# Attention 0 of a four-layer kernel: the gate's multiplication is moved from VectorE to GpSimd, with a second buffer

## The chip, the core and the metric

The kernel runs on one core of a Trainium2 chip. The metric is the device time of one execution in microseconds (us); the median of three runs is compared. In the rows of the profile the engines are PE (TensorE's matmuls), PEld (TensorE's weight loads), DVE (VectorE), ACT (ScalarE), POOL (GpSimd) and SP (SyncE).

## What is computed

The reference is a chain of four layers, each an attention and a feed-forward part, over 16 sequences of 256 rows with 128 channels. Only attention 0 and the first step of feed-forward 0 matter here:

```python
Q, K, V = (x @ Wq.T + bq), (x @ Wk.T + bk), (x @ Wv.T + bv)      # 16 heads of 64
scores = einsum('bnhd,bmhd->bhnm', Q, K) * (SCALE * adaptive_scale)
w = softmax(scores); attn = einsum('bhnm,bmhd->bnhd', w, V)
y = x + (attn @ Wo.T + bo)
x = layernorm(y) * gamma + beta        # the wrapper adds x and normalises once more
...
logits = einsum('td,ed->te', tokens, gate_w)      # feed-forward 0: 8 experts
```

The kernel works out these logits at the end of attention 0, on vector engines: each row of the new x (128 channels) times each of the 8 rows of gate_w, then a sum over the channels.

## The kernel before

Attention 0 is the function attention_wide. All float32. A batch is one sequence of 256 rows, that is two row tiles (t = 0, 1) of 128; a unit is a pair of heads of one batch, so there are 8 units in a batch and 128 in all. The engines run the same loop over **slots**, one slot for a unit, and each engine does in a slot what `at(slot, ...)` and `pair(slot, ...)` give it, in the order of its code. That order is the whole schedule: an engine that waits holds up all that stands behind it. With batch b, the offsets are

```python
LAG_T, LAG_PV, LAG_O = 2, 5, 6
X_AT, V_AT, Y_AT = -6, -1, U + 4
Z_AT, A_AT, W_AT = Y_AT + 4, Y_AT + 5, Y_AT + 8
G_AT = W_AT + 1
```

with U = 8, so Y_AT is 12, Z_AT 16, A_AT 17, W_AT 20 and G_AT 21.

- TensorE: in an even slot it scores two units (L272); in an odd slot it multiplies two units by V (L299) and then projects one quarter of a batch's V (L263, 64 of them, the last in slot 125). In each slot it turns a unit's probabilities (L285, unit slot-2) and projects Q and K of unit slot+2 (L255). Projections, turned x and the output projection (L307) all go through the one PSUM bank A_M; `bank_free` makes each wait until VectorE or ScalarE has emptied it. So the V projection of an odd slot waits for VectorE's take_qk (L410) of the even slot before it.
- VectorE, even slot: four row maxima (L399), then what falls due (take_y L429 with its moments L419/L422, write_x L448, inner_norm L437, outer_stats L419/L422), then take_qk (L410). Odd slot: the reciprocal of the even unit's sums (L404), take_turned (L415), take_qk (L410), the reciprocal of the odd unit's sums (L404). Behind that stand gate_x (L457, in slots 8b+21, +23, +25, +27, all odd) and sum_logits (L462, one slot later each).
- GpSimd, each slot: normalise (L185, four instructions for a unit, waits for the reciprocal). Behind it in odd slots: the reciprocal root of the first moments (root, L198/L200, slot 8b+15), add_biases of the next batch (L193, L194, slot 8b+17 counted from the batch before it) and affine (L205, L208, slot 8b+17), the root of the second moments (slot 8b+19).
- ScalarE: exponentials (L355), and copies out of PSUM.

Two places come up again. **Place A**, slot 8b+16: inner_norm (L437) waits for the root of slot 8b+15, and take_qk stands behind it. **Place B**, slot 8b+18: outer_stats (L419) waits for affine's last instruction (L208) of slot 8b+17, and take_qk stands behind it.

gate_x writes the one buffer `gated` (128 x 512) and waits until the sum before it has read it.

Of the kernel before, what the change touches and what calls it, by code (L numbers as in the profile page):

```python
# [9 lines left out]
ALU = mybir.AluOpType  # L10
ACT = mybir.ActivationFunctionType
AX = mybir.AxisListType
P = 128
H = 16
NB, SEQ = 16, 256
TB = SEQ // P
# [3 lines left out]
E = 8  # L20
# [30 lines left out]
def attention_wide(nc, name, x_state, x_rows, consts, w, dram, onward):  # L51
# [10 lines left out]
    G_AT = W_AT + 1  # L62
# [3 lines left out]
    with ExitStack() as ctx:  # L66
        def sb(n, shape, dt=F32):
            return ctx.enter_context(nc.sbuf_tensor(f"{name}_{n}", shape, dt))
# [17 lines left out]
        y, z, s = sb("y", [P, 2, TB, P]), sb("z", [P, 2, TB, P]), sb("s", [P, 2, TB, P])  # L86
        stats, mv, rstd = sb("stats", [P, 2, TB, 6]), sb("mv", [P, 2, TB, 2]), sb("rstd", [P, 2, TB])
        veps, mhalf = sb("veps", [P, TB]), sb("mhalf", [P, TB])
        gates, gated = sb("gates", [P, E, P]), sb("gated", [P, E // 2, P])
        CLEAR = 8  # L90
        CLEARS = max(TILES.values()) // CLEAR
        zeros, zeroed, cleared = sb("zeros", [P, CLEAR, P]), sem("zeroed"), sem("cleared")
# [4 lines left out]
        gate_done, lg_out = sem("gate_done"), sem("lg_out")  # L97
# [17 lines left out]
        def after(eng, signal, count):  # L115
            if count > 0:
                eng.wait_ge(signal, count)

        def at(s, offset, batches=NB):

            b, r = divmod(s - offset, U)
            return b if r == 0 and 0 <= b < batches else None
# [22 lines left out]
        def by_vector(n):  # L145

            return n % 2 == 1
# [6 lines left out]
        with nc.Block() as block:  # L154
# [19 lines left out]
            @block.gpsimd  # L174
            def _(pool):
                nc.gpsimd.memset(zeros[:], 0.0).then_inc(zeroed, 1)
                nc.gpsimd.memset(mhalf[:], -0.5).then_inc(set_up, 1)
                pool.wait_ge(set_up, 1)
                pool.wait_ge(in_rest, IN_REST)

                def normalise(n):
                    pool.wait_ge(inverted, n + 1)
                    for j in range(2):
                        for t in range(TB):
                            nc.gpsimd.tensor_scalar(prob[:, n % NP, j, t, :], prob[:, n % NP, j, t, :], rinv[:, n % NP, j, t:t + 1], 1.0,  # L185
                                                    ALU.mult, ALU.mult).then_inc(normed, 1)

                def add_biases(b):
                    pool.wait_ge(x_in[b // XB], 16)
                    after(pool, y_out, TB * (b - 1))  # L190
                    after(pool, s_out, TB * (b - 1))
                    xv = x_state[:, TB * b:TB * (b + 1), :]
                    nc.gpsimd.tensor_tensor(xb[:, b % 2], xv, bo[:].unsqueeze(1).to_broadcast([P, TB, P]), ALU.add).then_inc(xb_ready, 1)  # L193
                    nc.gpsimd.tensor_tensor(xbeta[:, b % 2], xv, beta[:].unsqueeze(1).to_broadcast([P, TB, P]), ALU.add).then_inc(xb_ready, 1)  # L194

                def root(b, moments, done):
                    pool.wait_ge(moments, 2 * TB * (b + 1))
                    nc.gpsimd.tensor_scalar(veps[:], mv[:, b % 2, :, 1], EPS, None, ALU.add).then_inc(done, 1)  # L198
                    pool.wait_ge(done, 2 * b + 1)
                    nc.gpsimd.tensor_tensor(rstd[:, b % 2], veps[:], mhalf[:], ALU.pow).then_inc(done, 1)  # L200

                def affine(b):
                    pool.wait_ge(z_out, TB * (b + 1))
                    pool.wait_ge(xb_ready, 2 * (b + 1))
                    nc.gpsimd.tensor_tensor(z[:, b % 2], z[:, b % 2], gamma[:].unsqueeze(1).to_broadcast([P, TB, P]), ALU.mult).then_inc(s_out, 1)  # L205
                    pool.wait_ge(s_out, TB * b + 1)
                    after(pool, x_done, TB * (b - 1))
                    nc.gpsimd.tensor_tensor(s[:, b % 2], z[:, b % 2], xbeta[:, b % 2], ALU.add).then_inc(s_out, 1)  # L208

                for slot in range(FIRST, LAST + 1):  # L210
                    if (n := pair(slot)) is not None:
                        normalise(n)
                    if (b := at(slot, Y_AT - 3)) is not None:
                        add_biases(b)
                    if (b := at(slot, Z_AT - 1)) is not None:
                        root(b, y_stats, rooted)
                    if (b := at(slot, A_AT)) is not None:
                        affine(b)
                    if (b := at(slot, W_AT - 1)) is not None:
                        root(b, s_stats, rooted2)  # L220
# [165 lines left out]
            def _(dve):  # L386
# [61 lines left out]
                        nc.vector.tensor_scalar(x_state[:, TB * b + t, :], s[:, b % 2, t, :], mv[:, b % 2, t, 0:1], rstd[:, b % 2, t:t + 1],  # L448
                                                ALU.subtract, ALU.mult).then_inc(x_done, 1)

                def gate_x(b, q):
                    t, some = q // 2, slice(E // 2 * (q % 2), E // 2 * (q % 2 + 1))
                    if b == 0 and q == 0:
                        dve.wait_ge(in_rest, IN_REST)
                    dve.wait_ge(x_done, TB * b + t + 1)
                    after(dve, lg_out, 2 * TB * b + q)
                    nc.vector.tensor_tensor(gated[:], x_state[:, TB * b + t, :].unsqueeze(1).to_broadcast([P, E // 2, P]), gates[:, some, :], ALU.mult).then_inc(gate_done, 1)  # L457

                def sum_logits(b, q):
                    t, some = q // 2, slice(E // 2 * (q % 2), E // 2 * (q % 2 + 1))  # L460
                    dve.wait_ge(gate_done, 2 * TB * b + q + 1)
                    nc.vector.tensor_reduce(onward["logit"][:, TB * b + t, some], gated[:], AX.X, ALU.add).then_inc(lg_out, 1)  # L462

                for slot in range(FIRST, LAST + 1):
                    if slot % 2 == 0:
                        for n in two(slot):
                            row_max(n, 0)
                            row_max(n, 1)
                    if slot % 2 == 1 and (n := pair(slot, 1)) is not None:
                        invert(n)  # L470
                    if (n := y_half(slot)) is not None:
                        take_y(n)
                    if (b := at(slot, W_AT)) is not None:
                        write_x(b)
                    if (b := at(slot, Z_AT)) is not None:
                        inner_norm(b)
                    if (b := at(slot, A_AT + 1)) is not None:
                        outer_stats(b)
                    if (n := pair(slot, LAG_T)) is not None and by_vector(n):
                        take_turned(n)  # L480
                    if (n := pair(slot, -QK_AHEAD)) is not None:
                        take_qk(n)
                    if slot % 2 == 1 and (n := pair(slot)) is not None:
                        invert(n)
                    for q in range(2 * TB):
                        if (b := at(slot, G_AT + 2 * q)) is not None:
                            gate_x(b, q)
                        if (b := at(slot, G_AT + 2 * q + 1)) is not None:
                            sum_logits(b, q)

# [2401 lines left out]
```

## Time and profile before

| | us |
|---|---|
| median of 3 runs | 2697.12 |
| lowest, highest | 2694.36, 2703.2 |
| the profiled execution | 2692.44 |
| its span in the profile | 2690.7 |
| span busy: TensorE matmul | 2248.2 (84%) |
| span busy: VectorE | 1593.5 (59%) |
| span busy: ScalarE | 1572.2 (58%) |
| span busy: GpSimd | 1361.9 (51%) |
| mean granted TensorE clock | 0.911 |

Attention 0 fills the first 684 us or so of the span: its last instruction, a sum of logits on VectorE, starts at 683.57. The timeline lists instructions of one engine in order of time, neighbours of one line merged with their count (x4), and in brackets how long the engine sat idle before and what ended that. The view of waits sums such idle times by pairs: who waited, for whom.

### The profile page before, as it was taken

To read this page: it belongs to the slowest core of one execution; us is meant where nothing else is said; L and a number is where in the kernel's file an instruction comes from. 1 tells how busy PE (TensorE), PEld (TensorE's weight loads), DVE (VectorE), ACT (ScalarE), POOL (GpSimd) and SP (SyncE) were. 2 spreads that over 40 slices of the span, in tenths; PEclk is the share of its full clock that TensorE was granted. 3 is DMA by queue.
4 is the path that set the end of the run, shared out by engine and by line. 5 is a ranking of instruction groups with operands and counts; after the bars stand their busy time and mean duration, and the time that the engine had idled before them with its cause. 6 is when DMAs were issued, how large, how long until landed. Compare 5 with 4: busy or idle time off the path is not lost. (4 is left out here: it accounts for less than half of the span.)

```text
span 2690.7 us, 52551 instructions
## 1 busy us (share of the span) xinstructions
PE 2248.2 (84%) x17832; PEld 1619.0 (60%) x17832; DVE 1593.5 (59%) x4357; ACT 1572.2 (58%) x3828; POOL 1361.9 (51%) x2164
## 2 busy tenths in 40 slices
PE   5999999998294899998399958999799699976783
PEld 3667667666193566665289934555345477754682
DVE  3566666666412899998623327667454466643465
ACT  3666666665152899998145524667544277651352
POOL 2454554555235888863133155654321488735346
PEclk9999999999596799999599969999899799987995
DMA  4000000000312322210311134332000333311232
GB/s 164 1 1 1 2 1 1 1 1 1 119 56 69 99 63 80 71 59 1 134 44 47 38 82 115 92 100 80 2 1 1 87 108 100 98 40 52 74 120 74
DMA packets 106506, 153.46 MB, mean 57 GB/s; under 512 B 17330, under 2 KB 78660, under 8 KB 99204
## 3 DMA queue, kind: packets, MB, share of 16 engines
q1 hardware_dynamic: 93956, 127.24, 15.3%
q0 software_dynamic: 12288, 22.86, 3.4%
q8 instruction: 148, 2.42, 0.4%
q14 instruction: 114, 0.93, 0.1%
HBM read 100.87 MB, written 47.19 MB: 55 GB/s over the span
## 5 line engine op out<-in xcount | busy, mean ns | idle before, releaser
L185 POOL TENSOR_SCALAR A_prob<-A_prob,A_rinv 128x256 f32<-128x256 f32 x512 | 254.3, 514 | 325.4 <-DVE A_rinv L404 325.4
L1011 DVE TENSOR_REDUCE A_nmax<-A_S 128x2 f32<-128x512 f32 (+1 forms) x512 | 311.5, 621 | 173.6 <-PE A_S L788 83.5
L940 ACT ACTIVATE A_PT<-A_E 128x512 f32<-128x512 f32 (+1 forms) x512 | 273.0, 551 | 142.3 <-PE A_E L811 65.8
L355 ACT ACTIVATE A_prob<-A_S,A_nmax 128x256 f32<-128x256 f32 x512 | 236.7, 488 | 102.9 <-DVE A_nmax L399 102.9
L1885 POOL DMA_INDIRECT L_xe<-rows,L_index x112 | 106.5, 950 | 231.3 <-PE L_k L1976 112.2
L1608 DVE TENSOR_SCALAR_CACHE_REDUCE A_D<-A_S 128x256 f32<-128x256 f32 x512 | 193.5, 417 | 14.8 <-PE A_S L1391 14.4
L1614 DVE COPY A_PT<-A_T 128x512 f32<-128x512 f32 x256 | 175.3, 687 | 19.4 <-PE A_T L1404 19.3
L1404 PE MATMUL A_T<-ident_sb,A_D 128*128 128x128 f32 x1024 | 160.5, 280 | 27.9 <-ACT A_D L1533 15.1
L2031 PE MATMUL L_k<-L_w,L_hT 128*128 (+1 forms) x1216 | 171.3, 279 | 12.3 <-ACT L_hT L2177 10.7
L2031 PEld LDWEIGHTS L_k<-L_w,L_hT 128*128 128x128 f32 x1216 | 153.8, 195 | 15.9 <-ACT L_hT L2177 12.6
L399 DVE TENSOR_REDUCE A_nmax<-A_S 128x2 f32<-128x512 f32 x256 | 158.7, 681 | 4.7 <-PE A_S L272 4.7
L255 PE MATMUL A_M<-A_xT,A_wqk 128*128 128x256 f32 x512 | 139.0, 394 | 14.8 <-ACT A_xT L341 12.3
L1404 PEld LDWEIGHTS A_T<-ident_sb,A_D 128*128 128x128 f32 x1024 | 116.7, 143 | 57.6 <-ACT A_D L1533 22.6
L1268 POOL TENSOR_TENSOR A_D<-A_D 128x1024 f32<-128x1024 f32 x64 | 120.6, 1891 | 47.1 <-ACT A_D L1528 47.0
L2017 PE MATMUL L_k<-L_xT,L_wr 128*128 128x128 f32 x896 | 131.2, 283 | 13.5 <-issue 9.7
L826 PE MATMUL A_O<-A_PT,A_v 128*32 128x256 f32 (+1 forms) x2048 | 140.2, 368 | 1.4 <-ACT A_OS L946 0.9
L285 PEld LDWEIGHTS A_T<-ident_sb,A_prob 128*128 128x128 f32 x1024 | 116.8, 141 | 40.1 <-issue 31.0
L2429 DVE TENSOR_TENSOR L_hT<-L_silus,L_k 128x512 f32<-128x512 f32 x72 | 49.5, 688 | 146.0 <-PE L_k L2021 76.5
L285 PE MATMUL A_T<-ident_sb,A_prob 128*128 128x128 f32 x1024 | 133.9, 274 | 0.3 <-ACT A_PT L361 0.3
L272 PE MATMUL A_S<-A_QK 64*128 64x256 f32 x1024 | 129.6, 393 | 0.0
L1528 ACT ACTIVATE A_D<-A_D 128x1028 f32<-128x1028 f32 x128 | 127.9, 1051 | 0.2
L299 PE MATMUL A_O<-A_PT,A_V 128*64 128x256 f32 x1024 | 124.9, 385 | 1.5 <-ACT A_OT L368 1.1
(426 smaller groups left out, 6036.9 us busy)
## 6 DMA issues: line engine op xcount, KB each, us to landing
A_QS<-stack_q SPq DMA_DIRECT2D x144, 192.0 KB
A_KS<-stack_k SPq DMA_DIRECT2D x144, 192.0 KB
results<-L_ye SPq DMA_DIRECT2D x48, 256.0 KB
stack_q<-A_parts SPq DMA_DIRECT2D x48, 192.0 KB
stack_k<-A_parts SPq DMA_DIRECT2D x48, 192.0 KB
L_w<-f_w SPq DMA_DIRECT2D x24, 256.0 KB, 6.9
sent<-A_zeros SPq DMA_DIRECT2D x10, 512.0 KB
L_xe<-sent SPq DMA_DIRECT2D x20, 256.0 KB
```

Source lines behind the costliest of these rows:

```text
L185: nc.gpsimd.tensor_scalar(prob[:, n % NP, j, t, :], prob[:, n % NP, j, t, :], rinv[:, n % NP, j, t:t + 1], 1.0, ALU.mult, ALU.mult).then_i ...
L255: i = nc.tensor.matmul(psM[:, j, :], wqk[:, j, g, :], xT[:, b % 2, :], start=True, stop=True)
L285: i = nc.tensor.transpose(psT[j][:, m, t * P:(t + 1) * P], prob[:, n % NP, j, t, m * P:(m + 1) * P], consts["ident"][:])
L355: nc.scalar.activation(prob[:, n % NP, j, t, :], psS[n % 2][j][:, t, :], ACT.Exp, bias=nmax[:, n % NP, j, t:t + 1], scale=1.0, accum_out=r ...
L399: nc.vector.tensor_reduce(nmax[:, n % NP, j, :], psS[n % 2][j][:], AX.X, ALU.max, negate=True).then_inc(maxed, 1)
L826: i = nc.tensor.matmul(psO[32 * j:32 * (j + 1), 0, n0:], v1[:, b % NV, m, h, :], p, start=(m == 0), stop=(m == TB - 1), skip_group_check=True)
L940: nc.scalar.activation(PT[:, n % RING, :], psE[n % 2][:, 0:BLOCKS, :].rearrange("p a b -> p (a b)"), ACT.Exp, scale=scale).then_inc(expd, 1)
L1011: nc.vector.tensor_reduce(nmax[:, b % 2, :, h], view, AX.X, ALU.max, negate=True).then_inc(maxed, 1)
L1404: i = nc.tensor.transpose(T[:, m, t * P:(t + 1) * P], D[:, u % RD, c:c + P], consts["ident"][:])
L1608: nc.vector.tensor_scalar(D[:, u % RD, c:c + SEQ], psS[n % 2][:, t, :], 1e-12, None, ALU.max, ALU.min, accum_out=D[:, u % RD, W + TB * j + ...
L1614: nc.vector.tensor_copy(PT[:, n % RP], psT[n % 2][:]).then_inc(turned_v, 1)
L2031: m = nc.tensor.matmul(psY[q % 2][:, k * P:(k + 1) * P], hT[:, i % HT, f, :], moving, start=(f == 0), stop=(f == NF - 1))
```

## The change

GpSimd gets gate_x: directly behind normalise in slots 8b+21, +23, +25 and +27 it multiplies, and ahead of add_biases, root and affine. The product goes to one of two buffers in turn, so that gate_x waits for the sum before the last one. VectorE keeps sum_logits, in the same slots.

```diff
-        gates, gated = sb("gates", [P, E, P]), sb("gated", [P, E // 2, P])
+        gates, gated = sb("gates", [P, E, P]), sb("gated", [P, 2, E // 2, P])
...
+                def gate_x(b, q):
+                    t, some = q // 2, slice(E // 2 * (q % 2), E // 2 * (q % 2 + 1))
+                    pool.wait_ge(x_done, TB * b + t + 1)
+                    after(pool, lg_out, 2 * TB * b + q - 1)
+                    nc.gpsimd.tensor_tensor(gated[:, q % 2], x_state[:, TB * b + t, :].unsqueeze(1).to_broadcast([P, E // 2, P]), gates[:, some, :], ALU.mult).then_inc(gate_done, 1)
+
                 for slot in range(FIRST, LAST + 1):
                     if (n := pair(slot)) is not None:
                         normalise(n)
+                    for q in range(2 * TB):
+                        if (b := at(slot, G_AT + 2 * q)) is not None:
+                            gate_x(b, q)
                     if (b := at(slot, Y_AT - 3)) is not None:
                         add_biases(b)
...
-                def gate_x(b, q):
-                    t, some = q // 2, slice(E // 2 * (q % 2), E // 2 * (q % 2 + 1))
-                    if b == 0 and q == 0:
-                        dve.wait_ge(in_rest, IN_REST)
-                    dve.wait_ge(x_done, TB * b + t + 1)
-                    after(dve, lg_out, 2 * TB * b + q)
-                    nc.vector.tensor_tensor(gated[:], x_state[:, TB * b + t, :].unsqueeze(1).to_broadcast([P, E // 2, P]), gates[:, some, :], ALU.mult).then_inc(gate_done, 1)
...
-                    nc.vector.tensor_reduce(onward["logit"][:, TB * b + t, some], gated[:], AX.X, ALU.add).then_inc(lg_out, 1)
+                    nc.vector.tensor_reduce(onward["logit"][:, TB * b + t, some], gated[:, q % 2], AX.X, ALU.add).then_inc(lg_out, 1)
...
-                        if (b := at(slot, G_AT + 2 * q)) is not None:
-                            gate_x(b, q)
```

GpSimd's program over six slots in the steady state of attention 0, from the root of slot 8b+15 to that of slot 8b+19. Before:

```order
L185 TENSOR_SCALAR A_prob<-A_prob,A_rinv 128x256 x16
L198 TENSOR_SCALAR A_veps<-A_mv 128x2
L200 TENSOR_TENSOR A_rstd<-A_veps,A_mhalf 128x2
L185 TENSOR_SCALAR A_prob<-A_prob,A_rinv 128x256 x8
L193 TENSOR_TENSOR A_xb<-x_state,A_bo 128x256
L194 TENSOR_TENSOR A_xbeta<-x_state,A_beta 128x256
L205 TENSOR_TENSOR A_z<-A_z,A_gamma 128x256
L208 TENSOR_TENSOR A_s<-A_z,A_xbeta 128x256
L185 TENSOR_SCALAR A_prob<-A_prob,A_rinv 128x256 x8
L198 TENSOR_SCALAR A_veps<-A_mv 128x2
L200 TENSOR_TENSOR A_rstd<-A_veps,A_mhalf 128x2
```

The same stretch in the changed kernel, where L214 is gate_x:

```order
L214 TENSOR_TENSOR A_gated<-x_state,A_gates 128x512
L198 TENSOR_SCALAR A_veps<-A_mv 128x2
L200 TENSOR_TENSOR A_rstd<-A_veps,A_mhalf 128x2
L185 TENSOR_SCALAR A_prob<-A_prob,A_rinv 128x256 x8
L214 TENSOR_TENSOR A_gated<-x_state,A_gates 128x512
L193 TENSOR_TENSOR A_xb<-x_state,A_bo 128x256
L194 TENSOR_TENSOR A_xbeta<-x_state,A_beta 128x256
L205 TENSOR_TENSOR A_z<-A_z,A_gamma 128x256
L208 TENSOR_TENSOR A_s<-A_z,A_xbeta 128x256
L185 TENSOR_SCALAR A_prob<-A_prob,A_rinv 128x256 x8
L214 TENSOR_TENSOR A_gated<-x_state,A_gates 128x512
L198 TENSOR_SCALAR A_veps<-A_mv 128x2
```

One multiplication now stands between the second normalise of each pair and the root, and one between normalise and the adds and affine.

VectorE's program over slots 8b+15 to 8b+18. Before:

```order
L404 RECIPROCAL A_rinv<-A_rsum 128x4
L457 TENSOR_TENSOR A_gated<-x_state,A_gates 128x512
L399 TENSOR_REDUCE A_nmax<-A_S 128x2 x4
L437 TENSOR_SCALAR A_z<-A_y,A_mv,A_rstd 128x128 x2
L410 TENSOR_TENSOR A_QK<-A_M,A_bqk 128x512
L462 TENSOR_REDUCE logit<-A_gated 128x4
L404 RECIPROCAL A_rinv<-A_rsum 128x4
L415 COPY A_PT<-A_T 128x512
L410 TENSOR_TENSOR A_QK<-A_M,A_bqk 128x512
L404 RECIPROCAL A_rinv<-A_rsum 128x4
L457 TENSOR_TENSOR A_gated<-x_state,A_gates 128x512
L399 TENSOR_REDUCE A_nmax<-A_S 128x2 x4
```

In the changed kernel the L457 rows are gone, and nothing else of this moves: the reciprocal that releases GpSimd stood ahead of the multiplication already.

## Rows read from the trace of the kernel before

**Rows 1.** Busy time by stretch, of 200 to 300 us (columns: PE, PEld, DVE, ACT, POOL).

```profile
200.00:300.00 100.00, 97.12 (x681) 70.06 (x680) 65.98 (x146) 66.55 (x222) 51.48 (x101) 1.00 0.00 1
```

**Rows 2.** Waits from 140 to 655 us: total us, times, longest us.

```profile
PEld A_M L263 <- DVE A_QK L410: 29.9, 26, 2.1
DVE A_stats L419 <- POOL A_s L208: 28.9, 13, 2.2
...
PE A_M L263 <- DVE A_QK L410: 19.0, 13, 1.7
...
DVE A_z L437 <- POOL A_rstd L200: 5.9, 13, 0.5
```

**Rows 3.** TensorE timeline: start us, us, line, idle before.

```profile
345.66 1.95 PE L299 MATMUL A_O<-A_PT,A_V 128*64 128x256 f32 x16
347.54 1.12 PE L263 MATMUL A_M<-A_wv,A_xT 128*128 128x512 f32 x2
...
357.85 1.13 PE L263 MATMUL A_M<-A_wv,A_xT 128*128 128x512 f32 x2 [1.45 <-DVE A_QK L410]
...
397.50 1.12 PE L263 MATMUL A_M<-A_wv,A_xT 128*128 128x512 f32 x2 [1.44 <-DVE A_QK L410]
```

**Rows 4.** VectorE timeline, slots 15 to 20 of one batch.

```profile
342.64 0.66 DVE L457 TENSOR_TENSOR A_gated<-x_state,A_gates 128x512 f32<-128x512 f32 x1
343.22 2.48 DVE L399 TENSOR_REDUCE A_nmax<-A_S 128x2 f32<-128x512 f32 x4
346.15 0.60 DVE L437 TENSOR_SCALAR A_z<-A_y,A_mv,A_rstd 128x128 f32<-128x128 f32 x2 [0.45 <-POOL A_rstd L200]
346.67 0.68 DVE L410 TENSOR_TENSOR A_QK<-A_M,A_bqk 128x512 f32<-128x512 f32 x1
...
356.50 0.49 DVE L419 BATCH_NORM_STATS2 A_stats<-A_s 128x6 f32<-128x128 f32 x2 [2.23 <-POOL A_s L208]
...
357.12 0.67 DVE L410 TENSOR_TENSOR A_QK<-A_M,A_bqk 128x512 f32<-128x512 f32 x1
...
365.03 0.60 DVE L448 TENSOR_SCALAR x_state<-A_s,A_mv,A_rstd 128x128 f32<-128x128 f32 x2
366.48 0.69 DVE L410 TENSOR_TENSOR A_QK<-A_M,A_bqk 128x512 f32<-128x512 f32 x1 [0.84 <-PE A_M L255]
```

**Rows 5.** GpSimd timeline of the same slots.

```profile
342.82 2.19 POOL L185 TENSOR_SCALAR A_prob<-A_prob,A_rinv 128x256 f32<-128x256 f32 x4 [2.32 <-DVE A_rinv L404]
...
345.41 0.71 POOL L200 TENSOR_TENSOR A_rstd<-A_veps,A_mhalf 128x2 f32<-128x2 f32 x1
...
351.39 2.19 POOL L185 TENSOR_SCALAR A_prob<-A_prob,A_rinv 128x256 f32<-128x256 f32 x4 [1.42 <-DVE A_rinv L404]
353.55 0.72 POOL L193 TENSOR_TENSOR A_xb<-x_state,A_bo 128x256 f32<-128x256 f32 x1
...
355.74 0.73 POOL L208 TENSOR_TENSOR A_s<-A_z,A_xbeta 128x256 f32<-128x256 f32 x1
...
364.28 0.71 POOL L200 TENSOR_TENSOR A_rstd<-A_veps,A_mhalf 128x2 f32<-128x2 f32 x1
```

**Rows 6.** Groups of instructions by line and shape, GpSimd, whole span.

```profile
L1268 POOL TENSOR_TENSOR A_D<-A_D 128x1024 f32<-128x1024 f32 x64 | 120.6, 1891 | 47.1 <-ACT A_D L1528 47.0
...
L1251 POOL TENSOR_TENSOR A_rest<-A_qk,A_parts 128x512 f32<-128x512 f32 x16 | 18.5, 1156 | 1.3
L208 POOL TENSOR_TENSOR A_s<-A_z,A_xbeta 128x256 f32<-128x256 f32 x16 | 12.0, 748 | 1.2
```

**Rows 7.** The multiplication on VectorE today, by line and shape.

```profile
L457 DVE TENSOR_TENSOR A_gated<-x_state,A_gates 128x512 f32<-128x512 f32 x64 | 43.0, 671 | 0.9
```

**Rows 8.** GpSimd timeline before the first gate multiplication.

```profile
113.76 1.84 POOL L185 TENSOR_SCALAR A_prob<-A_prob,A_rinv 128x256 f32<-128x256 f32 x4 [2.33 <-DVE A_rinv L404]
```

**Rows 9.** VectorE timeline at the end of attention 0.

```profile
677.00 0.60 DVE L448 TENSOR_SCALAR x_state<-A_s,A_mv,A_rstd 128x128 f32<-128x128 f32 x2
...
683.57 0.69 DVE L462 TENSOR_REDUCE logit<-A_gated 128x4 f32<-128x512 f32 x1
```


## The prediction

> **What bounds the kernel now.** I read the busy time by stretch first. In the steady state of attention 0 TensorE's matmuls fill 97 of 100 us, VectorE works 66 and GpSimd 51 [rows 1]. The change takes work off an engine with a third of its time free. So the question is not how much VectorE saves, but in which of TensorE's few idle stretches VectorE or GpSimd is the one waited for.
>
> The view of waits answers it for 140 to 655 us. TensorE's matmuls are idle for one thing of weight: the V projection waits for VectorE's take_qk, 13 times and 19.0 us, so 1.46 us each [rows 2]. In the same stretch VectorE itself waits 13 times for GpSimd's A_s, 2.2 us each, and 13 times for GpSimd's A_rstd, 0.45 us each [rows 2]. The thirteen are batches 1 to 13. The timelines of batch 6 (slots 63 to 68) put the three together, once for each place.
>
> Place B. VectorE's reciprocal releases GpSimd, which normalises from 351.39, adds from 353.55, and ends A_s at 355.74 + 0.73 = 356.47 [rows 5]. VectorE, idle for 2.23 us, takes its statistics at 356.50 and ends take_qk at 357.12 + 0.67 = 357.79 [rows 4]. The V projection starts at 357.85 after 1.45 us of idleness, and the next such one at 397.50, 39.65 us on [rows 3]. The chain runs reciprocal, GpSimd, VectorE, TensorE, and the first link hangs on TensorE: the take_qk that stands right ahead of that reciprocal in VectorE's program waits for TensorE's projection. So whatever is put into this chain is added to TensorE's time, once per batch.
>
> Place A, two slots earlier. GpSimd normalises from 342.82, and its root ends at 345.41 + 0.71 = 346.12 [rows 5]; VectorE starts inner_norm at 346.15 and ends take_qk at 346.67 + 0.68 = 347.35 [rows 4]. With the 0.06 us of hand-over seen at B, the V projection could have begun at 347.41, and it began at 347.54 [rows 3], when the matmuls before it were through. The slack here is 0.13 us. That TensorE's weight load waits 26 times for take_qk, twice as often as its matmuls [rows 2], says the same: this place is nearly late in each batch.
>
> **The change, part by part.**
>
> 1. 64 multiplications leave VectorE, 671 ns each, 43.0 us in all [rows 7]. In slots with row maxima behind them they cost 343.22 - 342.64 = 0.58 us from start to start [rows 4]. All of them stand behind the reciprocal that releases GpSimd, so no link of the two chains starts earlier. VectorE comes 0.58 us or less sooner to inner_norm and to the statistics, and waits there that much longer. Price on the path: 0.
>
> 2. 64 multiplications of 128 x 512 come to GpSimd. The trace has no such product with a broadcast operand, but it has the form: a float32 tensor_tensor of 128 x 512 takes 1156 ns; half of the 128 x 1024 one would be 946 ns, and two of 128 x 256 would be 1496 ns [rows 6]. I take 1.156, the row of the same size; neighbours overlap a little (normalise would end at 353.58 and the add starts at 353.55 [rows 5]), so 1.12 us in the chain, with bounds of 0.91 and 1.46.
> The GPSIMD Engine Reference of the Trainium skill, section on elementwise side-by-side accounting, speaks against this kind of move: a two-input elementwise operation is 1.96 times as long there as on VectorE. By that page the product would be an estimated 1.96 x 0.67 = 1.31 us, and the sum below some 4 us larger. I keep the row, which is 1.72 times VectorE's 671 ns.
>
> 3. GpSimd's normalise gets shorter. In odd slots its four instructions take 2.19 us now [rows 5], against 1.84 in a slot before the first multiplication ran on VectorE [rows 8]. VectorE's product starts at 342.64 and is still running when normalise starts at 342.82 [rows 4, 5], and the 0.35 us are about what is left of it. With the product gone from VectorE this comes back: -0.35 us in both chains. The other end is 0, if something else in odd slots is the cause.
>
> 4. So each chain grows by 1.12 - 0.35 = 0.77 us. At B all of it reaches TensorE: +0.77. At A the slack of 0.13 is used up first: +0.64. Together 1.41 us per batch, and the two add up, since each chain starts from TensorE's own progress. For 13 batches (batch 14's places lie behind slot 125, where no V is projected): **+18.3 us**.
>
> 5. The root of the second moments in slot 8b+19 is put off as well. It must be done when VectorE starts write_x at 365.03; take_qk behind it waits a further 0.84 us for TensorE [rows 4]. The root ends at 364.28 + 0.71 = 364.99 [rows 5]; 0.77 later, write_x ends at 366.4 instead of 365.63, still ahead of take_qk's 366.48. Cost 0, with 0.1 us to spare.
>
> 6. sum_logits could now wait for GpSimd. It stands behind row maxima and take_qk, and its product is ready within 1.84 + 1.12 us of the reciprocal, where the row maxima and take_qk alone take 2.48 + 0.68 [rows 4]. Cost 0. The two buffers and the sums that gate_x waits for lie two odd slots back. Normalise of the even units is released by VectorE later than GpSimd would be free, so it isn't pushed.
>
> 7. The end of attention 0. From the last write of x at 677.00 to the last sum at 683.57 + 0.69, VectorE alternates four products and four sums, 7.3 us [rows 9]. With two engines only the products are in a row: about 0.35 + 4 x 1.12 + 0.1 + 0.69 = 5.6 us, a gain of 1.6. Ahead of that, three insertions (root of batch 14, affine and second root of batch 15) delay the last x by 0.77 for the first and up to 0.5 for each other, since they partly fall into idle time. I book 0 and keep -1.6 and +1.8.
>
> The sum: 2692.44 for the profiled execution, of which 2690.7 is the span, plus 18.3 gives 2710.7. The profiled execution was 4.7 us under the median of the three runs; from that median the same step gives 2715.4. I take the middle, **2713.0 us**. With both low bounds (0.91 for the product) a batch costs 2 x 0.56 - 0.13 = 0.99, in all +12.9; with the product at 1.46 it is 2 x 1.11 - 0.13, +27; with 1.12 and no relief in normalise 2 x 1.12 - 0.13, +27 too.
>
> **The rivals.**
>
> *Nothing comes back to normalise, or the product is dearer.* Then each place grows by 1.12 to 1.46 less what comes back, the +27 above: 2719 to 2724. For it: item 3 is read only from the moment at which something happens.
> The skill's page on GpSimd, above, would put the product between the forecast and this case, an estimated 2715 to 2719; its ratio has no row here. Against it: the shorter normalise is exactly that of the slots without a product.
>
> *Only place B pays.* If the hand-over at A has more slack than the 0.13 us that I read from starts and modelled ends, 0.77 x 13 = +10, 2702 to 2707. For it: no matmul is shown idle there. Against it: the weight loads wait.
>
> *VectorE is what is late, not GpSimd* (the other side). If in slots 8b+16 and 8b+18 the row maxima behind the product are what take_qk really waits for, the products' 0.58 us comes off TensorE's 1.46 us of idleness in 13 batches, 7.5 us, and 1.6 at the end: 2683 to 2688. This decides only if GpSimd delivers A_s before VectorE is through its maxima. The four maxima take 2.48 us, and A_s comes 2.2 us after that, with the waits naming it [rows 2, 4]. It would have to come over 2 us sooner, and the change makes it later.
>
> *Nothing measurable*, within 0.3% (8 us, about what a measurement of this kernel can tell from no change): the low bound of the product and only place B, 0.56 x 13 = +7, or run-to-run differences over a real +13; the three runs shown differ by 8.8 us.
>
> **How the numbers follow.** The forecast (+12 to +22) has 0.62, the dearer case 0.14, only place B 0.10, nothing measurable 0.10, VectorE late 0.04. Of the place-B case and of the forecast's low end a little falls within 0.3%: same 0.12, slower 0.84, faster 0.04. The range takes in the place-B case and the dearer one, and the two bases 2692 and 2697: 2703 to 2726.
>
> **What would show it.** In the profile after: GpSimd's normalise 1.84 us in every slot; its product 1.1 to 1.2 us; VectorE's wait for A_s grown from 2.2 to about 3.4 us, and that for A_rstd from 0.45 to about 1.6 (0.77 later, and VectorE there 0.4 sooner); TensorE's wait in front of the V projection 26 times instead of 13, with 2.2 us at B and 0.6 at A; the period of a batch 41.1 us for 39.65; TensorE's busy share in the steady state down from 97 to about 93. The forecast is wrong if the wait at A doesn't appear or the one at B stays at 1.46; and if attention 0 ends some 18 us later but the whole is not longer, a later stage gave it back, for which I see no reason.

## The result, and the profile after

| | before | changed |
|---|---|---|
| median, us (4 runs each) | 2700.16 | 2732.08 |
| lowest to highest, us | 2694.36 to 2705.64 | 2727.07 to 2735.64 |
| span of the profiled execution, us | 2690.7 | 2733.9 |
| start of the last sum of logits, us | 683.57 | 712.94 |

The changed kernel is slower: the ratio is 1.011 with a 95% interval of 1.009 to 1.013, some +30 us; the medians differ by 31.9 us. The forecast was +18.3 us and the range ended at 2726; the direction and the places were right, the size was not. Attention 0 ends 29.4 us later. The 13.8 us that the span has on top of that lie in the later stages, which the change doesn't touch (2007.1 us behind the last sum before, 2021.0 now). That part varies from one execution to the next: on the two chips that ran the second and third set of experiments it was between 2018 and 2029 us long in eight profiled executions of kernels that differ in attention 0 alone.

The page's head for the changed kernel:

```profile
span 2733.9 us, 52549 instructions
...
PE 2267.3 (83%) x17832; PEld 1628.7 (60%) x17832; DVE 1561.6 (57%) x4293; ACT 1574.1 (58%) x3828; POOL 1421.7 (52%) x2228
```

GpSimd is some 60 us busier (81 for the products, 19 less for normalise), VectorE 32 us less busy. Neither matters as such. The view of waits, 140 to 675 us so that the same batches 1 to 13 are in it, where [rows 2] had 13 waits of matmuls for 19.0 us:

```profile
PEld A_M L272 <- DVE A_QK L419: 51.0, 26, 3.0
DVE A_stats L428 <- POOL A_s L208: 42.7, 13, 3.3
PE A_M L272 <- DVE A_QK L419: 39.2, 26, 2.5
...
DVE A_z L446 <- POOL A_rstd L200: 19.9, 13, 1.5
...
DVE x_state L457 <- POOL A_rstd L200: 11.0, 13, 0.9
```

TensorE now waits 26 times for take_qk (L419 here), 39.2 us. VectorE's two waits for GpSimd have grown by about 1.1 us each, and it waits for the second root as well. The timelines of batch 6, as in [rows 3 to 5]; first TensorE, place A, place B, and B of the next batch:

```profile
359.61 1.13 PE L272 MATMUL A_M<-A_wv,A_xT 128*128 128x512 f32 x2 [0.69 <-DVE A_QK L419]
...
370.77 1.12 PE L272 MATMUL A_M<-A_wv,A_xT 128*128 128x512 f32 x2 [2.31 <-DVE A_QK L419]
...
412.07 1.12 PE L272 MATMUL A_M<-A_wv,A_xT 128*128 128x512 f32 x2 [2.31 <-DVE A_QK L419]
```

GpSimd, place A and place B:

```profile
354.13 1.84 POOL L185 TENSOR_SCALAR A_prob<-A_prob,A_rinv 128x256 f32<-128x256 f32 x4 [2.31 <-DVE A_rinv L413]
355.93 1.27 POOL L214 TENSOR_TENSOR A_gated<-x_state,A_gates 128x512 f32<-128x512 f32 x1
...
357.60 0.71 POOL L200 TENSOR_TENSOR A_rstd<-A_veps,A_mhalf 128x2 f32<-128x2 f32 x1
...
363.46 1.84 POOL L185 TENSOR_SCALAR A_prob<-A_prob,A_rinv 128x256 f32<-128x256 f32 x4 [1.29 <-DVE A_rinv L413]
365.26 1.26 POOL L214 TENSOR_TENSOR A_gated<-x_state,A_gates 128x512 f32<-128x512 f32 x1
...
368.67 0.72 POOL L208 TENSOR_TENSOR A_s<-A_z,A_xbeta 128x256 f32<-128x256 f32 x1
```

VectorE, inner_norm at A, statistics at B, write_x two slots later:

```profile
358.35 0.60 DVE L446 TENSOR_SCALAR A_z<-A_y,A_mv,A_rstd 128x128 f32<-128x128 f32 x2 [1.53 <-POOL A_rstd L200]
...
369.43 0.49 DVE L428 BATCH_NORM_STATS2 A_stats<-A_s 128x6 f32<-128x128 f32 x2 [3.28 <-POOL A_s L208]
...
378.85 0.60 DVE L457 TENSOR_SCALAR x_state<-A_s,A_mv,A_rstd 128x128 f32<-128x128 f32 x2 [0.89 <-POOL A_rstd L200]
379.40 0.69 DVE L419 TENSOR_TENSOR A_QK<-A_M,A_bqk 128x512 f32<-128x512 f32 x1
```

Normalise takes 1.84 us where [rows 5] had 2.19. The product (L214) stands right behind it, 1.27 us long, and the root and the adds start only then. TensorE is idle for 0.69 us at A, where it was not, and for 2.31 us at B instead of 1.45. From B to B it is 41.30 us instead of 39.65 for this batch, and over the batches it is 41.29 us on average, the three below left out, instead of 39.67.

But three batches were longer still. From one B to the next it took 42.9 us behind the ones at 161.14, 245.33 and 494.65. TensorE's timeline behind the first, and the busy time by stretch, where the column behind POOL is the granted clock:

```profile
161.14 1.82 PE L272 MATMUL A_M<-A_wv,A_xT 128*128 128x512 f32 x2 [2.31 <-DVE A_QK L419]
162.75 1.92 PE L294 MATMUL A_T<-ident_sb,A_prob 128*128 128x128 f32 x8
```

```profile
150.00:160.90 10.90, 8.83 (x60) 6.05 (x60) 5.65 (x14) 7.03 (x25) 7.70 (x13) 1.00 0.01 2
160.95:164.36 3.41, 3.22 (x10) 2.14 (x11) 0.81 (x3) 1.11 (x3) 1.84 (x4) 0.57 0.00 0
164.40:174.00 9.60, 9.60 (x68) 7.00 (x67) 6.17 (x13) 5.61 (x21) 5.18 (x10) 0.98 0.00 0
```

The same two projections take 1.12 us elsewhere, and the eight transposes 1.04. The granted clock is 1.00 before and 0.57 in the stretch right behind TensorE's 2.31 us of idleness: most of it at the lower of the two levels (1.2 GHz in place of 2.4). In the kernel before, the granted clock is 1.00 from 140 to 660 us.

The end of attention 0, from the last long wait at B to the last sum, took 48.1 us before (635.51 to 683.57) and takes 51.6 now (661.36 to 712.94). These rows of TensorE's timeline carry most of it:

```profile
690.78 1.97 PE L308 MATMUL A_O<-A_PT,A_V 128*64 128x256 f32 x8 [1.84 <-issue]
693.77 3.72 PE L316 MATMUL A_M<-A_wo,A_OT 128*128 128x128 f32 x16 [1.02 <-ACT A_OT L377]
697.88 2.05 PE L316 MATMUL A_M<-A_wo,A_OT 128*128 128x128 f32 x16 [0.38 <-DVE A_y L438]
```

The first output projection of 16 matmuls takes 3.72 us, where it took 2.02 before, and the second 2.05 us. The products by V ahead of it take 1.97 us where they took 1.08 before. The busy time by stretch has the lower clock over just these groups:

```profile
690.50:697.30 6.80, 5.50 (x24) 4.33 (x24) 1.45 (x6) 0.84 (x2) 3.13 (x5) 0.50 0.00 0
697.40:700.00 2.60, 2.15 (x17) 1.86 (x16) 1.43 (x5) 0.00 (x0) 1.84 (x2) 1.00 0.00 0
```

In the kernel before, the clock is 1.00 from 660.00 to 670.10 us, over the same groups. In front of the products by V TensorE was idle for 1.84 us, against 0.40 in the kernel before. VectorE shows why; GpSimd has a product from 687.45 to 688.72:

```profile
687.51 1.97 DVE L446 TENSOR_SCALAR A_z<-A_y,A_mv,A_rstd 128x128 f32<-128x128 f32 x2 [4.32 <-POOL A_rstd L200]
...
690.00 0.68 DVE L424 COPY A_PT<-A_T 128x512 f32<-128x512 f32 x1
```

The copy of what these products read stands behind z, and ends 0.10 us before they start, as it does in the kernel before (663.40 and 663.50).

### The profile page after: what moved, and what is told of

Same layout as the page of the kernel before. It is cut to its first block and busy times, and to the rows that moved or that the text cites. A ratio compares the mean times of both kernels' runs of the same rounds, so it can differ in the third digit from the quotient of the medians.

```text
span 2733.9 us, 52549 instructions
## 1 busy us (share of the span) xinstructions
PE 2267.3 (83%) x17832; PEld 1628.7 (60%) x17832; DVE 1561.6 (57%) x4293; ACT 1574.1 (58%) x3828; POOL 1421.7 (52%) x2228
## 5 line engine op out<-in xcount | busy, mean ns | idle before, releaser
L185 POOL TENSOR_SCALAR A_prob<-A_prob,A_rinv 128x256 f32<-128x256 f32 x512 | 235.3, 478 | 304.5 <-DVE A_rinv L413 304.5
```

## The experiments

Theory 1 is that of the prediction: what stands in GpSimd's queue ahead of the root (A) and of affine (B) is added to TensorE's time, minus the slack at A, and minus 0.35 us that come back from normalise. The rival: GpSimd with its extra work is simply a worse place for the product, wherever it stands. A third question was the clock. Three chips were used, and the first of them ran the later stages faster (about 1902 us behind the last sum in e1), so kernels are compared by their ratio to the kernel before on the same chip. Four kernels ran on each: e1, e5_b, e5_a, e2; then e3, e6, e7, e8; then the changed kernel again, e4, e9, e10.

### Where the product stands in GpSimd's queue

All products as the last thing of their slots (e1), or only that of B (e5_b), or only that of A (e5_a):

```diff
                     if (n := pair(slot)) is not None:
                         normalise(n)
-                    for q in range(2 * TB):
-                        if (b := at(slot, G_AT + 2 * q)) is not None:
-                            gate_x(b, q)
...
                         root(b, s_stats, rooted2)
+                    for q in range(2 * TB):
+                        if (b := at(slot, G_AT + 2 * q)) is not None:
+                            gate_x(b, q)
```

> The changed kernel with GpSimd's products as the last thing of their slots, behind add_biases, affine and both roots. Theory 1 (what counts is what stands ahead of the root and of affine in GpSimd's queue): the wait at place A is gone, the one at B is 1.45 - 0.35 = 1.10 us, the period of a batch about 39.3 us, attention 0 some 5 us shorter than in the kernel before, the whole -4 to -7 us against it. Rival (GpSimd and VectorE simply have too much to do with the product on GpSimd, wherever it stands): it stays 20 us or more slower. On the clock: if the short stretches at half clock in the steady state come from the longer idle stretches of TensorE, there are none here.

> The changed kernel, but the product of slot 8b+25 (the one ahead of affine, place B) is put last in its slot; the other three stay. Theory 1: wait at B 1.10 us, at A 0.69 us as in the changed kernel, so +0.41 us per batch against the kernel before, period 40.1 us, +5 us in the steady state and +3 at the end: +6 to +10. Rival (load alone): as the changed kernel, +28 to +34. Clock: no stretch at half clock in the steady state, as no idle stretch of TensorE is longer than before.

> The changed kernel, but the product of slot 8b+23 (the one ahead of the first root, place A) is put last in its slot. Theory 1: no wait at A, at B 2.31 us, +0.87 us per batch, period 40.5 us: +11 in the steady state, +2 at the end, and up to three stretches at half clock at 1.6 us each: +12 to +19. If the sum of the single effects of A and B is not that of both (13 x 1.65 us without the clock's part), the two places act on each other.

| kernel | ratio to before (95%) | idle at A, us | idle at B, us | B to B at full clock, us | last sum starts, us |
|---|---|---|---|---|---|
| before | 1 | 0 | 1.45 | 39.67 | 683.57 |
| changed | 1.011 (1.009 to 1.013) | 0.69 | 2.31 | 41.29 | 712.94 |
| e1, all behind | 1.0005 (0.9997 to 1.0014) | 0.42 | 1.09 | 39.80 | 685.61 |
| e5_b, B's behind | 1.0025 (1.0014 to 1.0036) | 0.69 | 1.08 | 40.06 | 690.46 |
| e5_a, A's behind | 1.0093 (1.0077 to 1.0109) | 0.41 | 2.31 | 41.01 | 706.54 |

The rival is out: the same work on GpSimd costs 11 parts in a thousand or nothing, by its place in the queue. The two places add up, as item 4 of the prediction has it: from e1, the product ahead at A alone lengthens a batch by 0.26 us (e5_b), the one ahead at B alone by 1.21 (e5_a), and both by 1.49 (changed), where the sum of the two is 1.47. At B each kernel does what theory 1 says: 1.09 with the product behind, 2.31 with it ahead. e5_b came out as expected. At A it did not: with the product behind the root, TensorE should not have waited, and it waited 0.42 us. That made e1 level with the kernel before instead of 4 us faster, and e5_a dearer than its range. VectorE's timeline of e1 at place A, and GpSimd's:

```profile
186.88 1.55 DVE L446 TENSOR_SCALAR A_z<-A_y,A_mv,A_rstd 128x128 f32<-128x128 f32 x2 [0.31 <-POOL A_rstd L200]
```

```profile
186.12 0.72 POOL L200 TENSOR_TENSOR A_rstd<-A_veps,A_mhalf 128x2 f32<-128x2 f32 x1
186.81 1.28 POOL L214 TENSOR_TENSOR A_gated<-x_state,A_gates 128x512 f32<-128x512 f32 x1
```

The root releases inner_norm, and in the same moment GpSimd starts its product. The two z instructions then take 1.55 us instead of the 0.60 of [rows 4].

### VectorE and GpSimd at the same time

The product of slot 8b+23 moved past inner_norm, its sum put off by two slots (the rest as e1):

```diff
-                    for q in range(2 * TB):
-                        if (b := at(slot, G_AT + 2 * q)) is not None:
+                    for q, g_at in enumerate((G_AT, G_AT + 3, G_AT + 4, G_AT + 6)):
+                        if (b := at(slot, g_at)) is not None:
                             gate_x(b, q)
...
-                    for q in range(2 * TB):
-                        if (b := at(slot, G_AT + 2 * q + 1)) is not None:
+                    for q, s_at in enumerate((G_AT + 1, G_AT + 5, G_AT + 5, G_AT + 7)):
+                        if (b := at(slot, s_at)) is not None:
```

> The kernel with all products behind, but the one of slot 8b+23 goes to the end of GpSimd's slot 8b+24, after VectorE's z, and its sum to slot 8b+26. With the products behind, z took 1.55 us instead of 0.60 beside that product and TensorE waited 0.42 us at A. Theory 2 (the two engines can't run these two instructions at once): z is 0.60 us again, no wait at A, 1.10 us at B, period 39.3 us, 4 to 7 us less than the kernel before, where the version with the product beside z was level. If z stays long, something else stretches it.

Measured: ratio 0.9974 (0.9958 to 0.9989), so some 7 us less than the kernel before; no wait at A, 1.10 us at B, 39.32 us from B to B, last sum at 679.25. The instructions of L446 that write z, first in e1, then in this kernel (shortest, median, longest, ns):

```profile
L446 DVE TENSOR_SCALAR A_z<-A_y,A_mv,A_rstd x32: 333/556/1300, 107.8 to 675.1; 128x128 f32<-128x128 f32 x32
```

```profile
L446 DVE TENSOR_SCALAR A_z<-A_y,A_mv,A_rstd x32: 334/345/1285, 108.3 to 668.7; 128x128 f32<-128x128 f32 x32
```

The median is back at 345 ns. The longest is one at the end of attention 0, where a product still meets z. Over the kernels it follows the product's length: 1285 to 1307 ns where the product is 1.27 us long, 1174 in e9 with one of 1.16, 765 in e4 with one of 0.73 (both below). So VectorE waits for the whole of GpSimd's instruction. The other direction is item 3 of the prediction. A kernel without products on any engine (the sums read the gate's rows, the logits are left out):

```diff
-                    nc.vector.tensor_reduce(onward["logit"][:, TB * b + t, some], gated[:], AX.X, ALU.add).then_inc(lg_out, 1)
+                    nc.vector.tensor_reduce(onward["logit"][:, TB * b + t, some], gates[:, some, :], AX.X, ALU.add).then_inc(lg_out, 1)
...
-                        if (b := at(slot, G_AT + 2 * q)) is not None:
-                            gate_x(b, q)
```

> The kernel before without the products on any engine: the sums read the gate's rows instead, so the logits are left out. It measures by itself what VectorE's product costs. Theory 1: normalise takes 1.84 us in odd slots too, the wait at B is 1.10 instead of 1.45 us, 13 x 0.35 = 4.6 us, and some 3 us at the end of attention 0 where four products fall away: -7 to -9 us against the kernel before. If the 0.35 us has another cause than VectorE's product, only the 3 us at the end.

Measured: ratio 0.9976 (0.9967 to 0.9985), 6 us less, a little short of the -7 to -9 expected; 1.08 us at B, 39.30 us from B to B. In the profile the last sum ends 9.9 us earlier than in the kernel before, half of it from the steady state. Normalise's longest instruction is 482 ns, against 831 in the kernel before. And the opposite, VectorE's products kept and the same ones again on GpSimd:

```diff
+                def extra_gate(b, q):
+                    t, some = q // 2, slice(E // 2 * (q % 2), E // 2 * (q % 2 + 1))
+                    pool.wait_ge(x_done, TB * b + t + 1)
+                    after(pool, extra_done, 2 * TB * b + q - 1)
+                    nc.gpsimd.tensor_tensor(extra[:, q % 2], x_state[:, TB * b + t, :].unsqueeze(1).to_broadcast([P, E // 2, P]), gates[:, some, :], ALU.mult).then_inc(extra_done, 1)
...
+                    for q in range(2 * TB):
+                        if (b := at(slot, G_AT + 2 * q)) is not None:
+                            extra_gate(b, q)
```

> The kernel before, VectorE's products kept, and the same product once more on GpSimd where the change puts it (into tiles nobody reads). It doubles the suspected cost. Theory 1: both chains grow by the whole 1.23 us and nothing comes back from normalise, unless GpSimd's normalise and VectorE's product no longer meet: waits of TensorE 2.68 us at B and about 1.1 at A, +2.3 us per batch, +30 in the steady state. Theory on the clock (a stretch at half clock follows a long idle stretch of TensorE): three or more such stretches, at 1.6 us each, so +32 to +42 in all.

Measured: ratio 1.0175 (1.0143 to 1.0207), some +47 us; 1.04 us at A, 2.66 at B, 42.0 us from B to B at full clock, last sum at 732.65. That is more than the +32 to +42 expected: the steady state's 13 x 2.33 = 30.3 us are as forecast, but 8 intervals were some 1.55 us longer, 12.4 us, and the end of attention 0 took 6.7 us more. GpSimd's timeline at place A:

```profile
360.24 2.19 POOL L185 TENSOR_SCALAR A_prob<-A_prob,A_rinv 128x256 f32<-128x256 f32 x4 [2.31 <-DVE A_rinv L413]
362.40 1.26 POOL L214 TENSOR_TENSOR A_extra<-x_state,A_gates 128x512 f32<-128x512 f32 x1
...
364.06 0.71 POOL L200 TENSOR_TENSOR A_rstd<-A_veps,A_mhalf 128x2 f32<-128x2 f32 x1
```

Normalise is 2.19 us again, so it is VectorE's product that stretches it. The wait at B has grown by 1.21 us, the whole product from start to start, and the one at A from nothing to 1.04, the product less the slack.

This is a rule of the Trainium skill too. Its page SBUF — State Buffer, section "Who interferes with whom", says that GpSimd's ports to SBUF are a pair shared with VectorE, that a VectorE instruction with two SBUF inputs contends with a GpSimd instruction that reads SBUF, and that a tensor_scalar in a 2-port mode can contend too. It calls the pair an exclusive lock, and says of the 2-port mode that whoever issues first holds it for the whole instruction while the other is blocked. Both directions are seen here, with 0.35 us (GpSimd's normalise behind VectorE's product) and 0.95 us (VectorE's z behind GpSimd's product). In which mode z ran no run here shows.

### The length of the product

Half the product (two gate rows of four are left out, the sums read the first one four times), and the full one with its second operand in bfloat16 (the gate's rows are rounded):

```diff
-gated[:, q % 2], x_state[:, TB * b + t, :].unsqueeze(1).to_broadcast([P, E // 2, P]), gates[:, some, :], ALU.mult)
+gated[:, q % 2, 0:E // 4], x_state[:, TB * b + t, :].unsqueeze(1).to_broadcast([P, E // 4, P]), gates[:, half, :], ALU.mult)
```

```diff
+                nc.gpsimd.tensor_copy(gates_b[:], gates[:]).then_inc(gates_cast, 1)
...
-gates[:, some, :], ALU.mult)
+gates_b[:, some, :], ALU.mult)
```

> The changed kernel with GpSimd multiplying half as much (128 x 256; the other two gate rows of each product are left out, the sums read the first one four times). Dose for the chains: the product costs 0.68 us from start to start, so each chain grows by 0.68 - 0.35 = 0.33: TensorE idle 1.78 us at B, 0.20 at A, +0.53 us per batch against the kernel before: +7 in the steady state, +1 to +3 at the end: +7 to +11. A price that doesn't follow the product's length would stay at +20 or more. Clock: at most one stretch at half clock, as B's idle stretch is nearer to the 1.45 us that had none than to 2.31.

> The changed kernel with the gate's rows rounded to bfloat16 for GpSimd's product, x and the product still float32. The product was priced at 1.156 us and took 1.27. If the difference is the second operand's type (the row used for the price reads a bfloat16 second operand), it takes 1.16 us here, TensorE's idle stretches are 2.20 and 0.58 us, and the kernel is 3 us faster than the changed one. If it is the broadcast of x, the product stays at 1.27 us.

The products of the changed kernel, of e9 and of e4:

```profile
L214 POOL TENSOR_TENSOR A_gated<-x_state,A_gates x64: 1260/1269/1309, 135.9 to 711.6; 128x512 f32<-128x512 f32 x64
```

```profile
L217 POOL TENSOR_TENSOR A_gated<-x_state,A_gates_b x64: 1148/1155/1197, 136.4 to 708.3; 128x512 f32<-128x512 f32 x64
```

```profile
L215 POOL TENSOR_TENSOR A_gated<-x_state,A_gates x64: 723/729/761, 135.6 to 687.1; 128x256 f32<-128x256 f32 x64
```

With a bfloat16 second operand the product takes 1155 ns, the very price that the forecast had taken from L1251, whose second operand is bfloat16. With two float32 operands it takes 1269. TensorE's idle stretches at A and at B follow: 0.16 and 1.78 us in e4, 0.58 and 2.19 in e9, 0.69 and 2.31 in the changed kernel. e9 as a whole has the ratio 1.0086 (1.0058 to 1.0113) and its last sum at 709.47; the 3 us expected below the changed kernel are too little for the whole times to tell, whose intervals overlap. e4 takes 40.24 us from B to B and has its last sum at 687.83, 4.3 us behind the kernel before. Its whole time is 1.0001 (0.9983 to 1.0018), less than the +7 to +11 expected: the steady state's 7.5 us are there, the end of attention 0 gave some 3 back, and the rest is inside the interval.

### The clock

The changed kernel again, unchanged, beside these:

> The changed kernel once more, beside the next three and in a second profiled execution. The waits are the program's and should repeat: TensorE idle 2.31 us at B and 0.69 us at A, 41.30 us per batch at full clock. The stretches at half clock are the chip's: if they follow the long idle stretch at B, some appear again (one to five), each right behind a B and each worth about 1.6 us, but not behind the same batches. If there are none, the three of the first profile were chance and not part of the change. Whole: +26 to +33.

Measured: ratio 1.0108 (1.0079 to 1.0137); 0.70 and 2.32 us idle, 41.32 us from B to B, last sum at 711.39. Two intervals were 1.56 us longer, behind other Bs than in the first profile. What was expected of this run held in every point. Over all profiled executions, counting the intervals behind the Bs of batches 1 to 12 that are 1.5 us or more above the others:

| idle at B, us | kernels | longer intervals of 12 |
|---|---|---|
| none to 1.10 | e1, e2, e5_b, e6, e7, e8, e10 | 0 in each |
| 1.45 | before | 0 |
| 1.78 | e4 | 0 |
| 2.19 | e9 | 2 |
| 2.31 | changed, again, e5_a | 3, 2, 1 |
| 2.66 | e3 | 8 |

In e9 the B of batch 13, which isn't among the twelve, lost it as well: the granted clock is 0.50 from 657.00 to 660.30 us. Why one B loses the clock and the next doesn't, the profile doesn't tell; over the kernels, and within each of the three chips, more Bs lose it where the idle stretch ahead is longer. The stretch at A, 11 us before, is longer in most of these kernels too (0.16 us in e4, 0.41 in e5_a, 0.58 to 1.04 in the others); e5_b, with 0.69 us at A and 1.08 at B, lost nothing, so the stretch at A alone doesn't do it, but the share of the two isn't separated. At the end of attention 0 it is the same with the idleness in front of the last products by V. In six executions it is 1.14 to 2.18 us long (the changed kernel, its repetition, e9, e5_a, e5_b, e3), and all six have a projection of 3.65 to 3.75 us behind it. In the other eight it is 0.76 us or less, and the projection takes 2.02. That the idleness is the cause is argued from this order of cases and not shown; no run changed the clock by itself.

### A version that beats both

Where could GpSimd multiply for nothing? In the slots of a batch that neither root nor affine follows: 8b+20, 8b+21 and 8b+22, with four buffers (e6). But the product, 1.23 us from start to start, isn't the largest thing in B's chain that has no need to be there. That is add_biases, two instructions of 0.68 us from start to start, which stands ahead of affine by the accident of its slot. One slot later in the kernel before (e7), and both together (e8):

```diff
+                    for q, g_at in enumerate((G_AT - 1, G_AT, G_AT, G_AT + 1)):
+                        if (b := at(slot, g_at)) is not None:
+                            gate_x(b, q)
```

```diff
-                    if (b := at(slot, Y_AT - 3)) is not None:
+                    if (b := at(slot, Y_AT - 2)) is not None:
                         add_biases(b)
```

> The changed kernel with four product buffers and GpSimd's products in slots 8b+20, +21 (two) and +22, where neither root, affine nor z follow. Theory 2 (formed from the run with the products behind, in which z took 1.55 us instead of 0.60 while GpSimd's product ran): with the products ahead of nothing and beside no z, the wait at A is gone and the one at B is 1.10 us: period 39.3 us, -5 us in the steady state and -1 to -2 at the end: -5 to -8 against the kernel before. Rival (GpSimd's extra 81 us of work cost something anywhere): no faster than the kernel before.

> The kernel before with add_biases one slot later (8b+10), out of the chain of place B, products still on VectorE. Theory 1: the chain shrinks by 1.37 us (two instructions of 0.68 from start to start), TensorE's wait at B from 1.45 to under 0.1: 14 x 1.4 = 19 us: -17 to -20. If something else also holds VectorE's take_qk back at B, less.

> Both: the products on GpSimd in free slots and add_biases one slot later. Theory 1: no wait of TensorE for take_qk is left, period 38.2 us, -20 in the steady state and -1 to -3 at the end: -20 to -24, so only 2 to 5 us less than with add_biases alone, since the chains have slack then. If moving the product is worth something by itself once the chains are short, more.

| kernel | ratio to before (95%) | idle at B, us | last sum starts, us |
|---|---|---|---|
| e6, free slots | 0.9963 (0.9946 to 0.998) | 1.10 | 679.27 |
| e7, add_biases later | 0.9933 (0.9908 to 0.9959) | 0 | 665.19 |
| e8, both | 0.9928 (0.9906 to 0.995) | 0 | 664.57 |

Busy time by stretch over 140 to 620 us, in the kernel before and in e8 (columns PE, PEld, DVE, ACT, POOL):

```profile
140.00:620.00 480.00, 462.67 (x3218) 330.58 (x3216) 316.11 (x700) 321.78 (x1075) 251.43 (x484) 1.00 0.01 1
```

```profile
140.00:620.00 480.00, 479.49 (x3323) 341.44 (x3323) 302.93 (x676) 334.00 (x1116) 305.23 (x552) 1.00 0.01 1
```

The waits came out as expected, and so did the whole time of e7. e6 has 39.32 us from B to B, as forecast, and ends attention 0 by 4.3 us earlier; the -10 us of its ratio is beyond the -5 to -8 expected, but its interval, -5 to -15 us, takes most of that in. e8 was to gain 2 to 5 us over e7: its attention 0 is 0.6 us shorter, and the whole times can't tell the two apart. With add_biases out of the chain TensorE works 479.5 of 480 us in e8 (479.0 in e7), and attention 0 is 18 to 19 us shorter. So in free slots the products cost nothing on GpSimd, and once add_biases is out of the chain their move gains next to nothing either; the order of GpSimd's queue is what counts.

## Why the prediction was wrong, point by point

What bounds the kernel, and items 1, 5 and 6: right. No link of a chain started earlier; the second root, later by 0.9 us, used up the slack of write_x without reaching TensorE; VectorE waits for a product only four times, at the very end. In item 4 the places and the way they add up are right: both pay, and by their own progress, with 0.86 us more of idleness at B and 0.69 at A.

Item 2, the product's price, is the first term that was mis-sized: 1.156 us taken, 1.269 measured. The row had the right shape and a bfloat16 second operand, which e9 shows to be the whole difference. It costs 0.11 us at each place, 26 times, 3 us. The page that was set against it, the Trainium skill's GPSIMD Engine Reference, section "Elementwise — side-by-side cycle accounting", led to an estimate of 1.31 us and was nearer than my row: the 1.269 us are 1.89 times VectorE's 0.671, where the page has 1.96.

Item 3, the 0.35 us that come back: right in cause and size (e2, e3).

The steady state together, at full clock: 13 x 1.62 = 21.1 us (from 39.67 to 41.29 us a batch) against 18.3 forecast.

Left out of the forecast altogether: **the clock**. It treated a microsecond of TensorE's idleness as a microsecond. Three times in this profile the longer idle stretch was followed by one at the lower clock, 4.7 us in all, and once more at the end of attention 0.

Item 7, the end: booked at 0 with +1.8 as its upper end, measured +3.5. The last four products and sums did get shorter (from write_x to the last sum 6.1 us instead of 7.3), but TensorE waited 1.4 us longer in front of the last products by V (root 0.9 us late by the product, and z held up by the next one, 1.97 us for two instead of 1.43), and then those and the projection took 2.6 us more at the lower clock. The rest, 0.7 us, comes behind the last projection, where z meets a product again (1.54 us instead of 0.60) and the second root starts behind one.

21.1 + 4.7 + 3.5 = 29.3, against the 29.4 by which attention 0 ends later. The step that failed is the sum at item 4, "+18.3 us", taken as the whole cost: idle time of TensorE was priced as its own length, without the lower clock behind it, and that term, put at nothing, measured 4.7 us in the steady state and 2.6 at the end. The product's price (3 us) and the wait at the end (1.4 us) are the smaller parts of the miss. What the chip's clock does is measured here; that the longer idleness brings it down is argued.

Some of the miss is no fault of the mechanism. The 29.4 us on the median on record, 2697.12, would be 2726.5, just past the end of the range. The rest up to 2732.08 lies in later stages that the change doesn't touch, which the forecast took as fixed.

The rival "VectorE is what is late" is refuted by e1 and e5_a, in which VectorE has the same work and the wait at B goes by GpSimd's order; "only place B pays" by the 0.69 us at A; "nothing measurable" by the interval. "Nothing comes back, or the product is dearer" was nearer with its +27 us and had the right sign for the product, but that was luck in good part: the product was dearer by 0.11 us and not by 0.30, the 0.35 us did come back, and what filled the gap was the clock.

One thing was in hand and not used. At the end of attention 0 in the kernel before, VectorE's timeline has z long already, 1.43 us instead of 0.60, while GpSimd does its two adds (660.72 to 662.13):

```profile
660.78 1.43 DVE L437 TENSOR_SCALAR A_z<-A_y,A_mv,A_rstd 128x128 f32<-128x128 f32 x2 [2.85 <-POOL A_rstd L200]
```

That would have told that "put it behind the root" is no free place either.

## What to carry to other kernels

When work moves to an engine with idle time, list what stands behind it in that engine's queue and who waits for that; free time in another part of the period doesn't shorten that wait. Then look at what else stands ahead of the same instruction: here two adds nobody was waiting for cost 18 us of attention 0 (e7), where the products on VectorE cost 10 (e2). Price an instruction from a row with the same operand types, not only the same shape.

## What was not expected of the hardware

- Idle stretches of TensorE of 2.2 to 2.7 us, in a stage in which it is busy for 92% of the time, were followed by a lower granted clock in 1 to 8 of 12 cases, at some 1.56 us each; those of 1.78 us and less by none. At the end of the stage, where other idle stretches of about 1 us stand close by, those of 1.14 to 2.18 us were followed by it in all six cases. That the one brings the other is argued, as said above.
- A tensor_tensor of 128 x 512 on GpSimd takes 1269 ns with two float32 operands and 1155 ns with the second in bfloat16 (e9).
- VectorE's tensor_scalar with both its tensors in SBUF, 345 ns alone, takes about as long as the GpSimd product that it meets: 765, 1174 or 1285 ns beside products of 729, 1155 and 1273.
